# A graph layer and a mixture of experts on one core: an eighth of the edges' table rows fetched by TensorE instead of by GpSimd, with changes in the head, the router, the experts and the last stage

## The chip, the cores and the metric

The kernel runs on one core of a Trainium2 chip. The metric is the device time of one execution in microseconds (us), median of the runs. All data are float32 where nothing else is said.

## The reference, cut to what matters

x has 6250 nodes of 256 features, src and dst are 200,000 edges sorted by dst, edge_attr_2 gives two weights for each edge.

```python
def _L0_gnn_ref(h, adj, direction, W_forward, W_reverse, attn_forward):
    h_fwd = h @ W_forward.T                # 64 columns
    h_rev = h @ W_reverse.T                # 64 columns
    src, dst = (adj[0], adj[1])
    messages = h_fwd[src] * direction[:, 0:1] + h_rev[src] * direction[:, 1:2]
    scores = jnp.einsum('ef,hf->eh', messages, attn_forward[0])      # 4 heads
    scores = jax.nn.leaky_relu(scores, negative_slope=0.2)
    exp_scores = jnp.exp(scores - scores.max(axis=0, keepdims=True))
    sum_exp = jax.ops.segment_sum(exp_scores, dst, num_segments=N)
    norm = exp_scores / (sum_exp[dst] + 1e-10)
    outs = [jax.ops.segment_sum(messages * norm[:, hd:hd + 1], dst, num_segments=N) for hd in range(H)]
    return jnp.stack(outs, axis=1).reshape(N, -1)
...
x = x + _L0_gnn_ref(_layernorm(x), ...)
# 16 experts, the two best per node, hidden size 512, with biases, then a layer norm with gamma and beta
x = x + _L0_ffn_ref(_layernorm(x)[None], ...)[0]
```

## The kernel before

The work goes in five stages. TensorE, VectorE, ScalarE, GpSimd (with its own DMA queue) and SyncE (which issues most other DMAs) each run a hand-written list of instructions, ordered only by semaphores; the order in a list is the order in the code.

**Head** (`stage_edges`, first half, L211 to L622). The nodes are 49 tiles of 128 (NT). x is loaded to token_rows in eight parts, two in flight. For each tile TensorE transposes x (L397), ScalarE copies it (L330), TensorE multiplies it with the weights (L407), and ScalarE (L340) and VectorE (L505) in turn scale the product with 1/deviation to a row of 136 numbers: 64 and 4 (scores of the heads) for the forward matrix, the same for the reverse one. The tiles of a part are stored to the table in HBM, node_table, from two buffers. VectorE takes statistics (L482), converts dst and takes its ranges in each unit of 256 edges (L546 to L550) between the tiles. Behind the table it works out window starts in one partition (L569 to L622); the operation of L622 sets the semaphore `prepared`.

**Edges** (L625 to L851). 196 chunks (NCH) of 1024 edges, 8 columns (K) of 128 edges; four chunks (RING) are in flight. Per chunk: SyncE loads the indices; GpSimd issues eight indirect DMAs, one for each column, each of which gathers 128 rows of 136 numbers from node_table (L203 to L208, waiting at L705 to L707 for indices and for the buffer). ScalarE multiplies the reverse part (L723), VectorE the forward part (L770), both form scores (L773 to L787) and messages (L797), ScalarE the exponential (L728). VectorE forms a one-hot of the destination in a window of 16 nodes (hot, L779) and multiplies it with the exponentials (hot_ex, L801). TensorE sums a chunk's messages into 4 windows by 8 products (L688), which VectorE adds to the sums in SBUF (acc, L763) one chunk later, after it has loaded the windows' positions into registers. The loop body has four chunks.

**Nodes** (`stage_nodes`): seven groups of seven tiles: the sums are divided, x is added, a layer norm is made (xn), xn is transposed and multiplied with the gate weights, VectorE finds the two best experts and a slot for each (slot_i), and GpSimd scatters each row twice (98 indirect DMAs, L1011) to `dispatched` in HBM.

**Experts** (`stage_experts`): 104 tiles of 128 rows of one expert each; SyncE loads the expert's first weights, the rows xs (L1423) and the second bias, broadcast to all partitions (L1425); TensorE transposes (L1501) and makes both layers (L1512, L1522); VectorE adds the bias (L1577) and weighs (L1582); GpSimd scatters the result (L1375) to expert_rows.

**Last stage** (L1595 to L1747): for each group both rows of a node are loaded and added, normalised, scaled with gamma and stored, with two buffers; gamma is loaded behind the first group's rows (L1664).

## Time and profile before

| | |
|---|---|
| median of 3 runs | 2765.64 us (2764.18 to 2768.57) |
| the profiled execution: its own time | 2765.15 us |
| the profiled execution: span, first to last instruction | 2763.0 us |
| instructions | 40,902 |
| GpSimd busy | 1794.8 us |
| VectorE busy | 1178.0 us |
| TensorE busy (matmul) | 943.2 us |
| ScalarE busy | 757.5 us |
| HBM read, written | 222.54 MB, 38.69 MB |

The table by stretch gives busy times of each engine in a piece of the span, the granted clock of TensorE as a share of 2.4 GHz (0.50 is 1.2 GHz) and the mean load of the 16 DMA engines. The groups of instructions give, for one line of the kernel, the busy time and the mean duration of one, and the idle time of the engine just before them with what ended it. "PE" is TensorE, "PEld" its weight loads, "DVE" VectorE, "ACT" ScalarE, "POOL" GpSimd, "SP" SyncE; "issue" is time in which an engine waited for nothing that the profile shows.

### The profile page before, as it was taken

The numbers are of one execution on the slowest core, as the hardware profiler recorded it, in microseconds if no ns is written. First come the engines' busy times: TensorE is split into PE (matmuls) and PEld (weight loads), VectorE is DVE, ScalarE is ACT, GpSimd is POOL, SyncE is SP. The second block draws the span as 40 slices with busy tenths as digits, with TensorE's granted clock in tenths as the row PEclk, the third lists the DMA queues.
The fourth block names the chain that finished last, engine by engine and source line by source line (L and its number), as shares of the span: only waits on it lengthen the run. The fifth ranks groups of instructions, "written<-read, shape, count | busy, mean of one in ns | idle before, by whom it ended". The sixth has DMA issues, their size and how long they took to land.

```text
span 2763.0 us, 40902 instructions
## 1 busy us (share of the span) xinstructions
PE 943.2 (34%) x6693; PEld 862.8 (31%) x6694; DVE 1178.0 (43%) x4381; ACT 757.5 (27%) x2809; POOL 1794.8 (65%) x1923
## 2 busy tenths in 40 slices
PE   6311222222222211122222222211126559899860
PEld 6211111111111111111111111111126458888850
DVE  5533333333333333333333333333347656666646
ACT  3222222222222222222222222222234323333334
POOL 3677777777777777777777777777735643333326
PEclk8555555555555555555555555555555579999985
DMA  5222222222222222222222222222212667676656
GB/s 170 60 57 56 56 57 56 56 57 56 56 57 56 56 57 56 56 56 56 56 57 56 57 56 56 57 56 56 57 28 78 216 204 222 213 220 217 218 183 225
DMA packets 191305, 260.90 MB, mean 94 GB/s; under 512 B 64374, under 2 KB 133047, under 8 KB 191140
## 3 DMA queue, kind: packets, MB, share of 16 engines
q0 software_dynamic: 59872, 135.05, 19.8%
q1 hardware_dynamic: 124980, 122.05, 14.4%
q10 hardware_dynamic: 6416, 3.41, 0.4%
q8 instruction: 11, 0.18, 0.0%
q14 instruction: 26, 0.21, 0.0%
HBM read 222.54 MB, written 38.69 MB: 95 GB/s over the span
## 4 chain that ended last, share of the span: by engine, by line
POOL 53%; issue 21%; PE 8%; DMA 6%; DVE 5%; SPq 4%; ACT 2%; POOLq 1%; DVEq 0%; ACTq 0%
POOL rows L206 52%; DMA xs<-dispatched 4%; SPq L1366 3%; PE p_y L1522 2%; PE p_h L1512 2%; PE p_l L1093 1%; POOL dispatched L1011 1%; ACT xn L1043 1%; PE p_tab L407 1%; DMA shared<-expert_rows 1%; DMA dispatched<-xn,slot_i 1%; ACT staged L1027 1%; PE p_t L1108 1%; PE p_x L1501 0%; SPq L1416 0%
## 5 line engine op out<-in xcount | busy, mean ns | idle before, releaser
L206 POOL DMA_INDIRECT rows<-node_table,index x1568 | 1480.2, 944 | 533.0 <-issue 477.3
L688 PE MATMUL p_win<-hot_ex,msg 128*65 128x64 f32 x3136 | 393.8, 319 | 1559.2 <-DVE hot_ex L801 1170.5
L688 PEld LDWEIGHTS p_win<-hot_ex,msg 128*65 128x65 f32 x3136 | 359.6, 229 | 1593.3 <-issue 1187.6
L723 ACT ACTIVATE p_part<-rows,attr_all 128x64 f32<-128x64 f32 x1568 | 388.4, 299 | 1495.2 <-DMA rows<-node_table,index 1495.2
L770 DVE TENSOR_TENSOR part<-rows,p_attr 128x544 f32<-128x544 f32 x196 | 141.3, 721 | 870.4 <-DMA rows<-node_table,index 868.8
L763 DVE TENSOR_TENSOR shared<-shared,p_win 65x64 f32 x784 | 171.0, 218 | 394.4 <-issue 312.7
L1375 POOL DMA_INDIRECT expert_rows<-ys,back x104 | 102.0, 981 | 308.6 <-DVE ys L1582 240.9
L1512 PEld LDWEIGHTS p_h<-xt,shared 128*128 128x128 f32 x1664 | 203.4, 193 | 5.4
L1512 PE MATMUL p_h<-xt,shared 128*128 128x128 f32 x1664 | 203.9, 276 | 0.0
L1522 PE MATMUL p_y<-shared,hid_t 128*128 x832 | 197.6, 381 | 0.0
L1522 PEld LDWEIGHTS p_y<-shared,hid_t 128*128 128x128 f32 x832 | 149.9, 190 | 16.3
L1011 POOL DMA_INDIRECT dispatched<-xn,slot_i x98 | 99.4, 1014 | 77.2 <-issue 41.5
L797 DVE TENSOR_TENSOR msg<-part,p_part 128x512 f32<-128x512 f32 x196 | 132.6, 677 | 0.0
L801 DVE TENSOR_TENSOR hot_ex<-hot,p_ex 128x512 f32<-128x512 f32 x196 | 132.6, 677 | 0.0
L1467 ACT ACTIVATE hid_t<-p_h,shared 128x128 f32<-128x128 f32 x208 | 64.9, 363 | 174.2 <-PE p_h L1512 174.1
L1548 DVE TENSOR_SCALAR hid_t<-p_h,shared 128x128 f32<-128x128 f32 x208 | 63.4, 346 | 96.4 <-PE p_h L1512 94.6
L1577 DVE TENSOR_TENSOR p_y<-p_y,b_t 128x256 f32<-128x256 f32 x104 | 45.0, 432 | 54.6 <-PE p_y L1522 54.0
L1501 PE MATMUL p_x<-ident,xs 128*128 128x128 f32 x208 | 42.0, 284 | 70.8 <-DMA xs<-dispatched 70.8
L1485 ACT ACTIVATE own<-xs,is_first 128x256 f32<-128x256 f32 x104 | 52.6, 506 | 27.2 <-DVE is_first L1559 25.9
L1582 DVE SCALAR_TENSOR_TENSOR ys<-p_y,weight,own 128x256 f32<-128x256 f32 x104 | 50.3, 484 | 20.8 <-DVE p_y L1577 20.6
L1454 ACT ACTIVATE xt<-p_x 128x256 f32<-128x256 f32 x104 | 39.9, 383 | 62.8 <-PE p_x L1501 62.8
L779 DVE TENSOR_TENSOR hot<-dst_rel,p_dve 128x128 f32<-128x128 f32 x196 | 54.8, 280 | 0.0
(221 smaller groups left out, 1254.0 us busy)
## 6 DMA issues: line engine op xcount, KB each, us to landing
shared<-in_w SPq DMA_DIRECT2D x120, 512.0 KB, 6.3
rows<-node_table,index POOLq DMA_INDIRECT x1568
xs<-dispatched SPq DMA_DIRECT2D x104, 129.5 KB
b_t<-in_b SPq DMA_DIRECT2D x104, 128.0 KB, 4.1
shared<-expert_rows SPq DMA_DIRECT2D x14, 768.0 KB, 6.3
out<-shared SPq DMA_DIRECT2D x6, 896.0 KB, 4.1
token_rows<-in_x SPq DMA_DIRECT2D x5, 896.0 KB, 7.2
index<-in_src SPq DMA_DIRECT2D x196, 4.0 KB, 1.6
```

The costliest lines, as they stand in the source:

```text
L206: pool.indirect_dma_start(out=rows[:, s, k, :], out_offset=None, in_=table, in_offset=bass.IndirectOffsetOnAxis(ap=index[:, s, k:k + 1], a ...
L688: last = pe.matmul(psum[0:MSG, u * HEADS * W:(u + 1) * HEADS * W], msg[:, v, k, :], weighted[:, k, :, :].rearrange("p h w -> p (h w)"), st ...
L723: last = act.activation(p_part[:, v, k, :], rows[:, s, k, COLS:COLS + HD], ACT.Copy, scale=attr_all[:, 1, ds(c * K + k, 1)])
L763: return dve.tensor_tensor(to, to, psum.rearrange("p (h w) -> p h w", h=HEADS), ALU.add)
L770: dve.tensor_tensor(part[:, :, :], rows[:, s, :, 0:COLS], attr_p[:, 0, :].unsqueeze(2).broadcast_to([P, K, COLS]), ALU.mult)\
L797: dve.tensor_tensor(msg[:, v, :, 0:HD], part[:, :, 0:HD], p_part[:, v, :, :], ALU.add)\
L801: dve.tensor_tensor(hot_ex[:, v, :, :, :], hot[:, :, :].unsqueeze(2).broadcast_to([P, K, HEADS, W]), ex_p.unsqueeze(3).broadcast_to([P, K, ...
L1011: pool.indirect_dma_start(out=dispatched, out_offset=bass.IndirectOffsetOnAxis(ap=slot_i[:, v, n:n + 1], axis=0), in_=xn[:, v, n // 2, :], ...
L1366: return nc.values_load_multi_w_load_instructions(of[:, ds(i * R5 + first, n)], engines=[eng.engine], min_val=0, max_val=most)[1]
L1375: pool.indirect_dma_start(out=expert_rows, out_offset=bass.IndirectOffsetOnAxis(ap=back[:, r, :], axis=0), in_=ys[:, r, :], in_offset=None ...
L1512: last = pe.matmul(p_h[:, u, f // 2, (f % 2) * P:(f % 2 + 1) * P], w1_r[:, r % R5, c, f * P:(f + 1) * P], xt[:, u, c, :], start=(c == 0), ...
L1522: last = pe.matmul(p_y[:, u, 0:D], hid_t[:, u, c, :], w2_sb[:, ds(e, 1), c, :] .rearrange("p a d -> p (a d)"), start=(c == 0), stop=(c == ...
```

## The change

In the edge stage the eighth column (k = 7) of each chunk isn't gathered. The table stays in SBUF too (tab, in the memory of token_rows, 51 tiles of 136 numbers for each partition). SyncE writes the eighth column's sources, reduced to a third of the table, as `keys` to HBM once, and loads them for four chunks at a time, broadcast to all partitions. For each chunk VectorE compares the 128 keys with the node numbers of 17 tiles (GP = 17, onehot, 17 blocks of 128 x 128, in two pieces of 9 and 8 blocks). TensorE makes 17 products of a block with 3 x 136 = 408 columns of tab, all added up in one PSUM tile p_hot (`fetch`). The 408 columns are the row's candidates from the three thirds of the table. ScalarE writes the first, times a 0/1 mask, to the rows buffer (`keep_first`), VectorE adds the other two (`keep_others`). The last chunk gathers fewer columns. x is overwritten by this, so it is loaded again behind the last fetch.

Head: all tiles of the table stay in SBUF, x is loaded with four parts in flight, tiles are transposed in pairs and copied out in threes; the ranges of the destinations are made after the table; GpSimd makes keys and masks before it clears acc; 16 transposes of the identity run on TensorE at the start. Router: gate weights are centred, x before the layer norm is transposed and the logits are scaled with 1/deviation afterwards; the loop is unrolled, and the work of a group is spread otherwise. Experts: all second biases lie in SBUF, the 104 broadcasts of b2 go. Last stage: three load buffers, a first group of three tiles, three of seven additions on GpSimd instead of four of seven, other order.

```diff
-PARTS = [0, 2, 5] + [2 + U * m for m in range(1, NG)] + [NT]
+TRIPLE = 3
+PARTS = [0, 3] + list(range(6, NT, 6)) + [NT]
...
+KG = K - 1
+KG_LAST = -(-(EDGES - (NCH - 1) * CHUNK) // P)
+GP = -(-NT // 3)
+LEAD = 2
...
+        over_x = token_rows[:, :, :].rearrange("p t d -> p (t d)")
+        ends = [3 * GP * ROW, 3 * GP * ROW + 2 * GP * P, 3 * GP * ROW + 2 * GP * P + RING * P]
+        tab = over_x[:, 0:ends[0]].rearrange("p (t r) -> p t r", r=ROW)
+        onehot = over_x[:, ends[0]:ends[1]].rearrange("p (v g e) -> p v g e", v=2, g=GP)
+        key = over_x[:, ends[1]:ends[2]].rearrange("p (s e) -> p s e", s=RING)
...
-        def gather(pool, s):
-
-            for k in range(K):
+        def gather(pool, s, count=KG):
+
+            for k in range(count):
                 pool.indirect_dma_start(out=rows[:, s, k, :], out_offset=None, in_=table,
...
             @block.sync
             def _(sp):
                 def step(c, s, it, _):
-                    after(sp, gathered[s], 16 * K * it)
+                    after(sp, gathered[s], 16 * KG * it)
                     sp.dma_start(index[:, s, :], src[c] if isinstance(c, int)
                                  else src[ds(c, 1)].rearrange("a p k -> (a p) k")).then_inc(index_ready[s], 16)
 
-                chunks(sp, lambda it: None, step, RING)
+                def begin(it):
+
+                    if isinstance(it, int) and it == 0:
+                        return
+                    sp.wait_ge(hot_built, 2 * RING * it)
+                    of = keys[it * RING:(it + 1) * RING, :] if isinstance(it, int) else keys[ds(it * RING, RING), :]
+                    sp.dma_start(key[:, :, :], of.partition_broadcast(P)).then_inc(key_ready, 16)
+
+                chunks(sp, begin, step, RING)
...
              @block.scalar
             def _(act):
...
-                    act.wait_ge(gathered[s], 16 * K * (it + 1))
+                    act.wait_ge(gathered[s], arrived(c, s, it))
+                    act.wait_ge(hot_kept, 2 * (c + 1))
...
+                    if follows(c, 1):
+                        keep_first(c + 1, (s + 1) % RING)
+
+                def keep_first(c, s):
+
+                    act.wait_ge(hot_rows, c + 1)
+                    after(act, rows_used, c - RING + 1)
+                    act.activation(rows[:, s, KG, :], p_hot[:, 0:ROW], ACT.Copy, scale=third[:, 0, ds(c, 1)])\
+                       .then_inc(hot_third, 1)
...
              @block.tensor
             def _(pe):
...
+                    if follows(c, LEAD):
+                        fetch(c + LEAD, s % LEAD)
+
+                def fetch(c, v):
+
+                    after(pe, hot_kept, 2 * c)
+                    for gr in range(GP):
+                        if gr % HALF == 0:
+                            pe.wait_ge(hot_built, 2 * c + 1 + gr // HALF)
+                        last = pe.matmul(p_hot[:, 0:3 * ROW], onehot[:, v, gr, :], tab[:, gr:3 * GP:GP, :],
+                                         start=(gr == 0), stop=(gr == GP - 1))
+                    last.then_inc(hot_rows, 1)
...
              @block.vector
             def _(dve):
...
                     extra_windows(c, s, loaded[s])
+                    if follows(c, 1):
+                        keep_others(c + 1, (s + 1) % RING)
+                    if follows(c, LEAD):
+                        build_hot(c + LEAD, (s + LEAD) % RING, it + (s + LEAD) // RING)
+
+                def build_hot(c, s, it):
+
+                    dve.wait_ge(key_ready, 16 * (it + 1))
+                    after(dve, hot_rows, c - 1)
+                    for a, b in ((0, HALF), (HALF, GP)):
+                        dve.tensor_tensor(onehot[:, s % 2, a:b, :],
+                                          key[:, s, :].unsqueeze(1).broadcast_to([P, b - a, P]),
+                                          group_p[:, a:b].unsqueeze(2).broadcast_to([P, b - a, P]), ALU.is_equal)\
+                           .then_inc(hot_built, 1)
+
+                def keep_others(c, s):
+
+                    dve.wait_ge(hot_third, c + 1)
+                    row = rows[:, s, KG, :]
+                    for m in range(1, 3):
+                        after(dve, hot_kept, 2 * c + m - 1)
+                        dve.scalar_tensor_tensor(out=row, in0=p_hot[:, m * ROW:(m + 1) * ROW],
+                                                 scalar=third[:, m, ds(c, 1)], in1=row, op0=ALU.mult, op1=ALU.add)\
+                           .then_inc(hot_kept, 1)
...
 +            sp.wait_ge(g["hot_rows"], NCH)
+            for i in range(NG):
+                v, n = reloaded(i)
+                sp.wait_ge(v, n - 16)
+                if i == NG - 1:
+                    sp.wait_ge(s_hm, 1)
+                sp.dma_start(token_rows[:, i * U:(i + 1) * U, :],
+                             g["x"][i * U * P:(i + 1) * U * P, :].rearrange("(u p) d -> p u d", p=P)).then_inc(v, 16)
...
                     for c in range(KC):
                         last = pe.transpose(p_t[:, u % 2, c * P:(c + 1) * P],
-                                            xn[:, v, u, c * P:(c + 1) * P], ident[:, :])
+                                            tile_row(token_rows, t, c * P, P), ident[:, :])
...
 -                after(sp, s_ys, j - R5 + 1)
-                sp.dma_start(b2_t[:, r, :], g["b2"][ds(e, 1), :].rearrange("a d -> (a d)")
-                             .partition_broadcast(P)).then_inc(s_b2[r], 16)
...
-                dve.tensor_tensor(p_y[:, r % 2, 0:D], p_y[:, r % 2, 0:D], b2_t[:, r, :], ALU.add)\
+                dve.tensor_tensor(p_y[:, r % 2, 0:D], p_y[:, r % 2, 0:D], tile_row(b2_sb, e), ALU.add)\
                    .then_inc(s_biased, 1)
...
 +        LOADED, STORED, KEPT, SUMS = 3, 2, 4, 4
+        spots = [0, 3] + [3 + U * m for m in range(1, NG)] + [NT]
+        on_pool = [len(ts) * 3 // U for ts in tiles]
```

## Rows read from the trace of the kernel before

**Rows 1.** The page: busy times, and TensorE's clock in 40 slices

```profile
PE 943.2 (34%) x6693; PEld 862.8 (31%) x6694; DVE 1178.0 (43%) x4381; ACT 757.5 (27%) x2809; POOL 1794.8 (65%) x1923
...
PEclk8555555555555555555555555555555579999985
```

**Rows 2.** Busy time by stretch: stretch, length, engines, PEclk, DMA share, GB/s

```profile
500.00:1000.00 500.00, 100.44 (x800) 91.74 (x800) 174.54 (x601) 115.57 (x503) 378.10 (x401) 0.50 0.25 56
...
2300.00:2400.00 100.00, 90.72 (x619) 84.12 (x618) 62.96 (x264) 38.58 (x120) 32.54 (x36) 1.00 0.69 217
```

**Rows 3.** Groups by form, 1000 to 1100 us (line, busy, mean ns, idle before)

```profile
L206 POOL DMA_INDIRECT rows<-node_table,index x81 | 76.4, 943 | 24.7 <-issue 24.7
L723 ACT ACTIVATE p_part<-rows,attr_all 128x64 f32<-128x64 f32 x82 | 20.4, 299 | 76.7 <-DMA rows<-node_table,index 76.7
...
L763 DVE TENSOR_TENSOR shared<-shared,p_win 65x64 f32 x40 | 8.7, 218 | 20.1 <-issue 16.1
...
L801 DVE TENSOR_TENSOR hot_ex<-hot,p_ex 128x512 f32<-128x512 f32 x10 | 6.8, 677 | 0.0
L779 DVE TENSOR_TENSOR hot<-dst_rel,p_dve 128x128 f32<-128x128 f32 x11 | 3.1, 279 | 0.0
```

**Rows 4.** The chain that ended last, expert stage (start, us, what)

```profile
2243.10 1.73 PE p_y L1522 x8
2244.83 1.78 PE p_h L1512 x16
```

**Rows 5.** Instructions in order of time, end of the head

```profile
82.40 1.51 PE L440 MATMUL p_b<-lohi,ones 1*128 1x392 f32 x2
...
94.98 0.16 DVE L622 COPY neg_shift<-p_d 128x1 f32<-128x1 f32 x1 [0.67 <-PE p_d L448]
```

**Rows 6.** Groups by form, 0 to 80 us

```profile
L340 ACT ACTIVATE rows<-p_tab,rstd 128x136 f32<-128x136 f32 x25 | 9.3, 373 | 13.6 <-PE p_tab L407 7.6 <-DMA node_table<-rows 5.3
L505 DVE TENSOR_SCALAR rows<-p_tab,rstd 128x136 f32<-128x136 f32 x24 | 8.5, 354 | 21.3 <-DMA node_table<-rows 11.7 <-PE p_tab L407 9.4
```

**Rows 7.** Groups by form, 2260 to 2560 us

```profile
L1582 DVE SCALAR_TENSOR_TENSOR ys<-p_y,weight,own 128x256 f32<-128x256 f32 x72 | 34.8, 484 | 14.9 <-DVE p_y L1577 14.9
```

**Rows 8.** Instructions in order of time, one chunk of the edges

```profile
1004.27 0.68 DVE L801 TENSOR_TENSOR hot_ex<-hot,p_ex 128x512 f32<-128x512 f32 x1
...
1005.19 2.02 PE L688 MATMUL p_win<-hot_ex,msg 128*65 128x64 f32 x16 [8.13 <-DVE hot_ex L801]
```

**Rows 9.** Instructions in order of time, the last chunk

```profile
2040.14 0.72 DVE L770 TENSOR_TENSOR part<-rows,p_attr 128x544 f32<-128x544 f32 x1 [6.81 <-DMA rows<-node_table,index]
...
2048.07 1.27 DVE L763 TENSOR_TENSOR shared<-shared,p_win 65x64 f32 x4 [2.40 <-PE p_win L688]
```

**Rows 10.** GpSimd in order of time, first and last of 98 scatters

```profile
2086.18 1.03 POOL L1011 DMA_INDIRECT dispatched<-xn,slot_i  x1 [35.69 <-DVE slot_i L1189]
...
2226.13 0.97 POOL L1011 DMA_INDIRECT dispatched<-xn,slot_i  x1 [0.31 <-issue]
```

**Rows 11.** Waits from 2240 to 2670 us (total, times, longest)

```profile
PE p_x L1501 <- DMA xs<-dispatched: 37.1, 29, 1.8
```

**Rows 12.** The page: DMA issues (KB each, us to landing)

```profile
b_t<-in_b SPq DMA_DIRECT2D x104, 128.0 KB, 4.1
```

**Rows 13.** VectorE's waits from 2673 to 2763 us

```profile
DVE shared L1721 <- DMA gamma<-in_gamma: 12.5, 1, 12.5
```

**Rows 14.** Busy time by stretches of 5 us, head and expert stage (as rows 2)

```profile
55.00:60.00 5.00, 2.47 (x19) 1.95 (x18) 4.68 (x17) 1.91 (x7) 0.00 (x0) 0.96 0.25 75
60.00:65.00 5.00, 4.88 (x27) 4.64 (x28) 2.28 (x9) 2.52 (x7) 0.00 (x0) 0.69 0.08 25
...
2235.00:2240.00 5.00, 3.42 (x15) 3.02 (x16) 0.00 (x0) 2.03 (x3) 0.00 (x0) 0.50 0.47 128
2240.00:2245.00 5.00, 5.00 (x37) 4.79 (x36) 2.33 (x16) 2.57 (x10) 0.00 (x0) 0.92 0.64 156
...
2275.00:2280.00 5.00, 3.16 (x24) 2.83 (x24) 3.88 (x18) 1.50 (x5) 2.36 (x3) 1.00 0.70 219
```

More of the change, by code:

```diff
@@ L386, in _, with transpose, product @@
                 last.then_inc(s_wp, 1)
+                def transpose(q):
+                    after(pe, s_xtc, q - 2)
+                    for t in pair(q):
+                        pe.wait_ge(s_x[part_of[t] % 4], 16 * (part_of[t] // 4 + 1))
+                        for c in range(KC):
+                            at = (t % 2) * D + c * P
+                            last = pe.transpose(p_xt[:, q % 3, at:at + P], token_rows[:, t, c * P:(c + 1) * P],
+                                                ident[:, :])
+                    last.then_inc(s_xt, 1)
+                def product(t):
+                    q, j, m = t // 2, t // TRIPLE, t % TRIPLE
+                    pe.wait_ge(s_xtc, q + 1)
+                    if t == 0:
+                        pe.wait_ge(s_wd, 2)
+                    if m == 0 and j >= 3:
+                        copies, n = copied(j - 2)[0 if by_act(j) else 1]
+                        pe.wait_ge(copies, n)
+                    for c in range(KC):
+                        last = pe.matmul(p_tab[:, j % 3, m * ROW:(m + 1) * ROW], x_tr[:, q % 3, t % 2, c, :],
+                                         w_all[:, c, :], start=(c == 0), stop=(c == KC - 1))
+                    if t == triple(j)[-1]:
+                        last.then_inc(s_tab, 1)
+                transpose(0)
                 pe.wait_ge(s_ident, 3)
@@ L1057, in deviation @@
                 act.activation(rstd[:, :], mv[:, :, 1], ACT.Sqrt, bias=eps[:, 0:1]).then_inc(s_sd, 1)
-            stage(0)
+            stage(0, 0, U)
+            transposed(0)
+            stage(1, 0, GB)
             deviation(0)
-            alternate(act, step)
-            totals(NG - 1)
+            normalised(0, 0, 0)
+            unrolled(act, step)
         @block.tensor
         def _(pe):
+            pe.wait_ge(s_in, 32)
+            for c in range(KC):
+                last = pe.matmul(p_n[:, 0, 0:E], ones[:, :], gate_w_sb[:, c, :], start=(c == 0), stop=(c == KC - 1))
+            last.then_inc(s_gs, 1)
             pe.wait_ge(s_hm, 1)
@@ new lines, in store @@
+            def store(n):
+                sp.wait_ge(s_f, spots[n + 1])
+                for a, b, real in pieces(n):
+                    sp.dma_start(dram(g["out"], a, b, real),
+                                 out_rows[0:real, n % STORED, a - spots[n]:b - spots[n], :])\
+                      .then_inc(s_out[n % STORED], 16)
+            sp.wait_ge(returned, 1)
+            load(0)
+            sp.dma_start(gamma[:, :], g["gamma"].partition_broadcast(P)).then_inc(s_g, 16)
+            for n in range(1, LOADED):
+                load(n)
@@ L1673, in _ @@
+            for n in range(count):
+                if n + LOADED < count:
+                    load(n + LOADED)
+                store(n)
+            for n in range(count - STORED, count):
+                sp.wait_ge(s_out[n % STORED], stored(n))
         @block.scalar
         def _(act):
[L1675 to L1679 removed]
@@ new lines, in _ @@
+            act.wait_ge(returned, 1)
+            act.activation(table_for[:, :], eps[:, :], ACT.Sqrt)
+            second_rows(0)
+            deviation(0)
+            for n in range(count):
+                if n + 1 < count:
+                    second_rows(n + 1)
+                act.wait_ge(s_rc, 2 * n + 2)
+                for t in tiles[n]:
+                    u = t - spots[n]
+                    after(act, s_gm, t - KEPT + 1)
+                    act.activation(p_norm[:, t % KEPT, 0:D], y0[:, n % LOADED, u, :], ACT.Identity,
+                                   bias=nmr[:, n % 2, u:u + 1], scale=rstd[:, n % 2, u:u + 1]).then_inc(s_nm, 1)
+                if n + 1 < count:
+                    deviation(n + 1)
```

786 lines of the change are left out of this document (436 added, 350 removed).

## The prediction, made before the kernel was run

> **What bounds the kernel now.** First the page's busy shares and its 40 slices [rows 1]: GpSimd is busy 65% of the span, TensorE 34%, and in the long middle TensorE shows 1 to 2 tenths at half clock (1.2 GHz) and GpSimd 7. The table by stretch [rows 2] shows what the stages are made of: the edges run from 95 to 2049 us [rows 5, 9], then nodes, experts and the last stage take 714 us together. In 500 us of edges GpSimd is busy 378 us and TensorE 100; in experts TensorE is busy 91 us of 100 at full clock (2.4 GHz). The groups of the edge stage [rows 3] say why GpSimd's 76% is its limit: 81 gathers in 100 us, 0.943 us each with 0.305 us of issue between them, 1.248 us a gather, 8 gathers or 9.985 us a chunk. The other engines wait for the gathered rows (ScalarE 76.7 us of 100), and TensorE waits for them in turn. 196 chunks of 9.985 us are 1957 us, and the measured stage has 1954 [rows 5, 9]. So the edges cost 71% of the time, and a gather less per chunk is worth something, if nothing slower takes its place.
>
> **The edges after the change.** Removed: one gather of eight per chunk, 1.248 us x 196 = 244 us on the engine that is now the limit. GpSimd would need 8.74 us a chunk.
>
> Added on TensorE, for each chunk: fetch, 17 products (GP) of a 128x128 one-hot block with 408 columns (3 x 136) of the table, all f32. An f32 product leaves two matmul records in this trace: 4 calls of 256 columns are 8 records in 1.73 us and 8 calls of 128 columns 16 records in 1.78 us, both at full clock [rows 4]. That is 0.216 us per record of 256 columns, 0.845 ns a column. The widest f32 products of the trace, 392 columns at half clock, take 0.85 us a record (two in 1.51 us) [rows 5]: 1.65 ns a column from start to start plus 0.2 us until the end, so twice the above at half the clock. A record of 408 columns is then 0.345 us at full clock, a call 0.69, and a fetch 34 x 0.345 + 0.2 = 11.9 us. This alone is more than the whole chunk costs now (9.985 us). 196 x 11.9 = 2332 us against a stage of 1954.
>
> Can it lie beside the other work? PSUM has one p_hot. The chain from one fetch to the next, by the code: the last product ends; ScalarE copies the first third (136 columns with a scale from PSUM, 0.373 us [rows 6]); VectorE adds the other two thirds, two dependent operations of 136 columns (0.484 us is the one of this form with 256 columns; 120 columns fewer at 1.04 ns are 0.36 [rows 7]); then VectorE, in its own order, builds the next one-hot block, first 9 groups, 1152 elements: hot_ex has 512 elements in 0.677 us and hot 128 in 0.279, so 1.04 ns an element, 1.34 us [rows 3]; then TensorE starts, 0.23 us after VectorE's end as in a chunk now [rows 8]. With 0.04 us at each of three hand-overs and 0.08 of overlap between VectorE's operations: 0.04 + 0.37 + 0.04 + 0.36 + 0.04 + 0.36 - 0.08 + 1.34 + 0.23 = 2.7 us. TensorE's window products (2.0 us a chunk at half clock [rows 8], about 1.1 at full) fit in these 2.7 us; the second 8 groups (1.2 us of VectorE) are built during the first 9 products. **Period: 11.9 + 2.7 = 14.6 us.**
>
> What stays hidden, by what: VectorE has 3.5 us of old work a chunk [rows 2] plus 0.7 and 2.6, in all 6.8 of 14.6; its word load and waits (1.6 us before the four windows [rows 3]) fit in the 11.9 us of a fetch. ScalarE's 8 copies (2.4 us) too. SyncE moves the keys once in four chunks, 256 KB after the fourth build, with a fetch of 11.9 us before they are wanted; the 128 KB broadcast of b2 takes 4.1 us [rows 12], so twice that at worst still fits. Behind this wait on SyncE stand the four index loads, and behind them GpSimd; it has 5.8 us to spare in each period. If the cover of 2.7 us is too thin for windows, branch and the word load in every fourth chunk, it costs up to 1 us a chunk; below, a gap of 2.0 us is the least I can make of the three drains and the build. So the period is between 13.9 and 15.6.
>
> Sum of the stage: first build 1.4 and a first fetch that starts at half clock 14.0 (see the clock below), second fetch 13.2, 194 periods 2832, then the last row's thirds 1.2 and a last chunk as now, 9.2 us [rows 9]: 2871 us for 1954. **+917 us** (bounds +780 and +1110).
>
> **The other parts.** Head: VectorE waits 11.7 us for table stores and 9.4 for products [rows 6]; the new head keeps all tiles of the table in SBUF, so the first wait goes, and part of the second by copies of three tiles at once; but the ranges of the destinations, now made between the tiles, move behind the table. -12 (between -25 and +8). Nodes: 98 scatters from 2086.2 to 2227.1, at 0.97 and 0.31 us of issue each 125 of 141 us [rows 10]; the router starting from unnormalised rows can win the rest and a few us of start, while x comes in again behind the last fetch under a tail of 10 us: -15 (-30 to +10). Experts: without the b2 broadcast, 104 transfers of 128 KB fewer; TensorE waits 37.1 us in all for xs [rows 11], of which I take 15 (0 to -37). Last stage: its start waits 12.5 us for gamma behind the first loads [rows 13]; small first group and third buffer: -10 (0 to -20). Together **-52**.
>
> 2763 + 917 - 52 = 3628 us of span. The profiled execution took 2765.15 with a span of 2763.0, half a microsecond from the median of 2765.64, so 2.6 are added: **3630 us**.
>
> **One rule against the trace.** In the expert stage the clock rose after some 4.2 us of busy TensorE (3.42 in one stretch, 0.8 in the next, whose mean is 0.92), and then stayed at full through a stretch of 5 us with 1.84 us idle; in the head, after a stretch with 2.5 us idle in 5, the mean fell to 0.69 [rows 14]. The new gap has 1.6 us without products (2.7 less 1.1) and 13 us of products around it, so I take full clock throughout. The Trainium skill, TensorE: Matmul & The Clock Gate, section on a second HAM failure mode, reports a kernel in which short idles between groups of matmuls, as buffers in PSUM went round, brought the clock down again and again. By that rule each fetch here would begin slow, which is the first rival below.
>
> **The rivals.**
> (1) The clock falls in each gap. Each fetch then has 4.2 us at half clock and loses 2.1 us: 194 x 2.1 = 407, **4040 us**. For it: the fall in the head [rows 14]. Against: the expert stage, whose idles are as long, keeps full clock.
> (2) The clock stays at half in the edges, as it does now [rows 2]. A fetch is 34 x 0.68 + 0.2 = 23.3, the period 26.1, 194 x 11.5 = 2231 more: **5870 us**. Against: TensorE is then busy over 90%, more than in the stretch where it rose.
> (3) The other side: faster. Its place is the fetch on TensorE: if the products with a one-hot block took much less than the two passes of 0.845 ns a column that the rows show, for instance one short pass, and a fetch came under 8.74 - 2.7 = 6.0 us (0.35 us a call), the gathers would bound again: 196 x 8.74 = 1713, -244 - 52, **2470 us**. It breaks even at a period of 10.2 us, a fetch of 7.5 us or 0.44 us a call. Against: 0.69 us a call by two shapes at full clock [rows 4], and the blocks and the table are declared f32.
> That the change doesn't do what it says I give nothing of its own: only the eighth column is fetched in the new way, and the gathers are counted in a loop.
>
> **How the numbers follow.** Forecast 0.83 (own range 3440 to 3850, from the bounds of the stage, less or more the small parts), rival (1) 0.08, (2) 0.05, (3) 0.03, and 0.01 for something that ends within 0.2%, about what a measurement of this kernel can tell from no change. The range 3440 to 4050 takes in rival (1) and leaves out some 0.15. Faster 0.03, same 0.01, slower 0.96.
>
> **What would show it.** GpSimd with 7 gathers a chunk and idle after them, waiting for used rows; TensorE about 87 to 90% busy through the edges at clock 1.0, with 34 records of 408 columns a chunk of some 0.35 to 0.5 us recorded; fetch to fetch 14.6 us, with 2.7 us between, and one-hot builds of 1.34 and 1.2 us; node stage starting near 2950. In the chain, TensorE's fetch line with some 60% of the span instead of GpSimd's gather with 52%. Wrong it would be if the records of 408 columns are spaced under 0.22 us (3), if the clock in the edges is 0.5 (2) or between (1), or if the gap between fetches is over 4 us, which would mean a wait that I haven't seen (keys, or VectorE's old work before the thirds).

## The result and the profile after

The changed kernel takes 3886.56 us (median of 4 runs, 3884.60 to 3886.97) against 2765.66 us: a ratio of 1.4045, interval 1.4023 to 1.4067. The forecast was 3630 us, with a range of 3440 to 4050; the result lies in the range, between the forecast and rival (1), but outside the forecast's own range of 3440 to 3850. The profiled execution has a span of 3882.8 us, 1119.8 more than the kernel before.

Where the time went is read off the boundaries between the stages, in the order of time (start, us, engine, line, operation, and in brackets the idle time before it with what ended it). The end of the head:

```profile
88.12 0.16 DVE L695 COPY neg_shift<-p_tab 128x1 f32<-128x1 f32 x1 [0.67 <-PE p_tab L536]
```

The last addition of a window, which ends the edges:

```profile
3217.30 1.27 DVE L894 TENSOR_TENSOR shared<-shared,p_win 65x64 f32 x4 [2.23 <-PE p_win L781]
```

The first and the last of the 98 scatters of the node stage:

```profile
3247.17 1.04 POOL L1187 DMA_INDIRECT dispatched<-xn,slot_i  x1 [27.45 <-DVE slot_i L1387]
...
3375.26 0.98 POOL L1187 DMA_INDIRECT dispatched<-xn,slot_i  x1 [0.30 <-issue]
```

The first product of the experts, and the last scatter of the experts:

```profile
3392.21 1.11 PE L1699 MATMUL p_x<-ident,xs 128*128 128x128 f32 x4 [48.17 <-DMA xs<-dispatched]
```

```profile
3805.64 0.98 POOL L1576 DMA_INDIRECT expert_rows<-ys,back  x1 [0.94 <-issue]
```

Against the same boundaries of before [rows 5, 9, 10]; its first product of the experts and their last scatter are these:

```profile
2234.92 0.69 PE L1501 MATMUL p_x<-ident,xs 128*128 128x128 f32 x2 [32.10 <-DMA xs<-dispatched]
```

```profile
2673.51 0.97 POOL L1375 DMA_INDIRECT expert_rows<-ys,back  x1 [0.75 <-issue]
```

| stage | before | after | difference | forecast |
|---|---|---|---|---|
| head, to the end of L622 / L695 | 95.1 | 88.3 | -6.9 | -12 |
| edges, to the last window added | 1954.2 | 3130.3 | **+1176** | +917 |
| nodes, to the experts' first product | 185.6 | 173.6 | -12 | -15 |
| experts, to the start of their last scatter | 438.6 | 413.4 | -25 | -15 |
| last stage | 89.5 | 77.2 | -12 | -10 |

So the four small parts give back 56 us, near the 52 forecast, and the whole difference to the forecast lies in the edges. The page of the changed kernel (busy shares, the clock in 40 slices, and the groups that answer to [rows 1, 3]):

```profile
PE 3292.4 (85%) x13377; PEld 2057.2 (53%) x13378; DVE 1756.7 (45%) x5176; ACT 842.2 (22%) x2982; POOL 1608.7 (41%) x1726
...
PEclk8999999999999999999999999999999995599996
...
L873 PE MATMUL p_hot<-token_rows 128*128 128x408 f32 x6664 | 2553.9, 546 | 383.4 <-DVE token_rows L950 382.1
...
L236 POOL DMA_INDIRECT rows<-node_table,index x1368 | 1291.5, 944 | 1839.3 <-DMA index<-in_src 1400.4
L961 DVE SCALAR_TENSOR_TENSOR rows<-p_hot,third,rows 128x136 f32<-128x136 f32 x392 | 140.7, 359 | 1452.8 <-ACT rows L839 1393.0
L839 ACT ACTIVATE rows<-p_hot,third 128x136 f32<-128x136 f32 x196 | 73.2, 373 | 2099.7 <-PE p_hot L873 2099.7
L950 DVE TENSOR_TENSOR token_rows<-token_rows,p_dve 128x1152 f32<-128x1152 f32 (+1 forms) x392 | 485.2, 1280 | 0.0
```

TensorE is busy 85% instead of 34% and its clock is 8 to 9 tenths in the edges, not 5 and not 10. L873 is `fetch`: 196 x 34 = 6664 records, as forecast, but of 546 ns each in the mean; in the second and third experiment below, at full clock throughout, it is 510 and 509. GpSimd (L236) has 1368 gathers instead of 1568 and waits between them, so it bounds nothing now; its waits are put down to the indices, but SyncE issues these behind the keys, which wait for the fourth build, and so go at the pace of the fetches. The idle time before a fetch, 383.4 us, has VectorE's one-hot build (L950) as its releaser, 196 times 2.0 us. The table by stretch, 500 us of the edges (columns as [rows 2]):

```profile
500.00:1000.00 500.00, 439.26 (x1566) 250.23 (x1565) 204.62 (x509) 85.67 (x343) 210.47 (x223) 0.93 0.15 35
```

The clock is 0.93 and TensorE has no product in 61 us of 500. That is neither the forecast (1.00) nor rival (2) (0.50). One chunk of the loop in order of time, from the start of a fetch to the start of the next:

```profile
1503.97 13.60 PE L873 MATMUL p_hot<-token_rows 128*128 128x408 f32 x34 [1.89 <-DVE token_rows L950]
...
1517.41 1.11 PE L781 MATMUL p_win<-hot_ex,msg 128*65 128x64 f32 x16
...
1517.87 0.37 ACT L839 ACTIVATE rows<-p_hot,third 128x136 f32<-128x136 f32 x1 [11.24 <-PE p_hot L873]
...
1518.52 0.36 DVE L961 SCALAR_TENSOR_TENSOR rows<-p_hot,third,rows 128x136 f32<-128x136 f32 x1 [8.02 <-ACT rows L839]
1519.03 0.36 DVE L961 SCALAR_TENSOR_TENSOR rows<-p_hot,third,rows 128x136 f32<-128x136 f32 x1 [0.15 <-DVE rows L961]
1519.31 2.48 DVE L950 TENSOR_TENSOR token_rows<-token_rows,p_dve 128x1152 f32<-128x1152 f32 x2
...
1520.70 1.64 PE L873 MATMUL p_hot<-token_rows 128*128 128x408 f32 x3 [2.18 <-DVE token_rows L950]
```

This fetch takes 13.60 us, the pause without products before it was 1.89 us, the one before the next 2.18 us. From the last product to the third on ScalarE, to VectorE's two thirds, to the build, to TensorE: the chain is the one forecast, in this order. Between the end of ScalarE's copy (1518.24) and VectorE's first third lie 0.28 us, and 0.15 us between the thirds. In time order again, the last four chunks, which aren't in the loop, so that every address is a constant:

```profile
3182.02 11.88 PE L873 MATMUL p_hot<-token_rows 128*128 128x408 f32 x34 [1.66 <-DVE token_rows L950]
...
3193.74 1.11 PE L781 MATMUL p_win<-hot_ex,msg 128*65 128x64 f32 x16
...
3193.95 0.37 ACT L839 ACTIVATE rows<-p_hot,third 128x136 f32<-128x136 f32 x1 [9.35 <-PE p_hot L873]
...
3194.35 0.75 DVE L961 SCALAR_TENSOR_TENSOR rows<-p_hot,third,rows 128x136 f32<-128x136 f32 x2 [6.02 <-ACT rows L839]
3195.02 2.48 DVE L950 TENSOR_TENSOR token_rows<-token_rows,p_dve 128x1152 f32<-128x1152 f32 x2
...
3196.51 3.66 PE L873 MATMUL p_hot<-token_rows 128*128 128x408 f32 x10 [1.66 <-DVE token_rows L950]
```

Here the fetch takes 11.88 us, the two thirds run back to back in 0.75, the pause is 1.66 us and the period from fetch to fetch 14.49: the forecast's 11.9, 1.6 and 14.6. The records say what the other 1.7 us of the loop's fetch are. TensorE in stretches of half a microsecond around the start of that fetch (busy us, clock, DMA share, GB/s):

```profile
1503.50:1504.00 0.50, 0.03 (x1) 1.00 0.63 139
1504.00:1504.50 0.50, 0.50 (x2) 0.96 0.01 0
1504.50:1505.00 0.50, 0.50 (x2) 0.50 0.34 78
...
1507.50:1508.00 0.50, 0.50 (x2) 0.63 0.20 44
1508.00:1508.50 0.50, 0.50 (x2) 1.00 0.00 0
```

Products stop at 1502.08 and start at 1503.97. In the first half microsecond of the fetch the clock is 0.96 in the mean, then 0.50, in the last stretch but one 0.63, then full again: some 3.4 us at 1.2 GHz, which cost 1.7. Over the whole stage, 128 of 194 fetches have such a stretch and take 13.6 us, and 66 take 11.9. In all 128 the clock falls 0.1 to 1.4 us behind the fetch's first product, and not in the pause itself. The mean period is 15.93 us.

### The profile page after: what moved, and what is told of

Read it like the earlier page. It is cut to its first block, busy times and chain, and to the rows that moved or that the text cites. A ratio compares the mean times of both kernels' runs of the same rounds, so it can differ in the third digit from the quotient of the medians.

```text
span 3882.8 us, 56640 instructions
## 1 busy us (share of the span) xinstructions
PE 3292.4 (85%) x13377; PEld 2057.2 (53%) x13378; DVE 1756.7 (45%) x5176; ACT 842.2 (22%) x2982; POOL 1608.7 (41%) x1726
## 4 chain that ended last, share of the span: by engine, by line
PE 68%; DVE 16%; issue 6%; DVEq 4%; ACT 3%; SPq 1%; DMA 1%; ACTq 0%; POOL 0%; POOLq 0%
PE p_hot L873 64%; DVE token_rows L950 7%; DVE rows L961 2%; DVEq L1567 2%; ACT rows L839 2%; DVE p_y L1774 1%; PE p_h L1710 1%; SPq L1142 1%; PE p_y L1720 1%; DVE second L1754 1%; DVEq L961 1%; DVE hid_t L1746 1%; DVE back L1759 1%; PE p_tab L488 0%; DMA out<-shared 0%
## 5 line engine op out<-in xcount | busy, mean ns | idle before, releaser
L873 PE MATMUL p_hot<-token_rows 128*128 128x408 f32 x6664 | 2553.9, 546 | 383.4 <-DVE token_rows L950 382.1
L873 PEld LDWEIGHTS p_hot<-token_rows 128*128 128x128 f32 x6664 | 1345.5, 204 | 1490.8 <-issue 1092.7
L236 POOL DMA_INDIRECT rows<-node_table,index x1368 | 1291.5, 944 | 1839.3 <-DMA index<-in_src 1400.4
L961 DVE SCALAR_TENSOR_TENSOR rows<-p_hot,third,rows 128x136 f32<-128x136 f32 x392 | 140.7, 359 | 1452.8 <-ACT rows L839 1393.0
L839 ACT ACTIVATE rows<-p_hot,third 128x136 f32<-128x136 f32 x196 | 73.2, 373 | 2099.7 <-PE p_hot L873 2099.7
L950 DVE TENSOR_TENSOR token_rows<-token_rows,p_dve 128x1152 f32<-128x1152 f32 (+1 forms) x392 | 485.2, 1280 | 0.0
L781 PEld LDWEIGHTS p_win<-hot_ex,msg 128*65 128x65 f32 x3136 | 217.0, 139 | 75.6 <-issue 69.6
L781 PE MATMUL p_win<-hot_ex,msg 128*65 128x64 f32 x3136 | 217.8, 223 | 5.8 <-DVE msg L930 5.8
L1720 PEld LDWEIGHTS p_y<-shared,hid_t 128*128 128x128 f32 x832 | 150.0, 190 | 16.9 <-issue 0.9
L902 DVE TENSOR_TENSOR token_rows<-rows,p_attr 128x544 f32<-128x544 f32 x196 | 140.3, 716 | 1.7 <-issue 1.6
L930 DVE TENSOR_TENSOR msg<-token_rows,p_part 128x512 f32<-128x512 f32 x196 | 132.7, 677 | 0.0
```

Source lines behind the costliest of these rows:

```text
L236: pool.indirect_dma_start(out=rows[:, s, k, :], out_offset=None, in_=table, in_offset=bass.IndirectOffsetOnAxis(ap=index[:, s, k:k + 1], a ...
L781: last = pe.matmul(psum[0:MSG, u * HEADS * W:(u + 1) * HEADS * W], msg[:, v, k, :], weighted[:, k, :, :].rearrange("p h w -> p (h w)"), st ...
L839: act.activation(rows[:, s, KG, :], p_hot[:, 0:ROW], ACT.Copy, scale=third[:, 0, ds(c, 1)])\
L873: last = pe.matmul(p_hot[:, 0:3 * ROW], onehot[:, v, gr, :], tab[:, gr:3 * GP:GP, :], start=(gr == 0), stop=(gr == GP - 1))
L902: dve.tensor_tensor(part[:, :, :], rows[:, s, :, 0:COLS], attr_p[:, 0, :].unsqueeze(2).broadcast_to([P, K, COLS]), ALU.mult)\
L930: dve.tensor_tensor(msg[:, v, :, 0:HD], part[:, :, 0:HD], p_part[:, v, :, :], ALU.add)\
```

## The experiments

Theory A, of the 259 us that the edges take beyond the forecast: two things lengthen the period, and nothing else. The masks of the thirds are addressed by a register in the loop (`third[:, m, ds(c, 1)]`), which stretches the hand-overs of ScalarE and VectorE and so the pause; and TensorE's clock falls behind most of these pauses. Theory B: something else holds the chain up (keys, VectorE's old work, the build), and the clock only follows it.

**Is it the clock?** Five products that nobody reads, into a free part of the other window tile, behind each chunk's window products:

```diff
+                    for _ in range(5):
+                        pe.matmul(p_win[:, 1 - v, 384:512], ones[:, :], ident[:, :], start=True, stop=True)
                     if follows(c, LEAD):
                         fetch(c + LEAD, s % LEAD)
```

> Edit: after the window sums of each chunk TensorE makes five more f32 products of the ones and the identity (128 columns each, into an unused part of the other p_win bank, read by nobody), so that its pause before the next fetch shrinks from 1.9 us to about 0.9. Theory A: the clock falls in two fetches of three because TensorE pauses 1.9 us and more before each; with shorter pauses every fetch takes 11.9 us instead of 13.6 in 128 of 194, the period is 14.8 us and the time 3887 - 218 = 3670 us. Theory B: the clock falls for another reason (the long load itself, the gathers beside it); then two thirds of the fetches still take 13.6 us and the time stays at 3887, or above it if the products delay the fetch.

Measured: 3671.47 us (3670.93 to 3671.95), ratio 1.3268 [1.3248, 1.3289]. In order of time:

```profile
1509.11 1.11 PE L781 MATMUL p_win<-hot_ex,msg 128*65 128x64 f32 x16
...
1510.05 1.33 PE L865 MATMUL p_win<-ident,ones 128*128 128x128 f32 x10
...
1512.11 11.91 PE L875 MATMUL p_hot<-token_rows 128*128 128x408 f32 x34 [0.72 <-DVE token_rows L952]
```

The ten records of L865 add 1.33 us of work on TensorE, leave a pause of 0.72 us, and the kernel is 215 us faster. All 194 fetches take 11.9 us, and the mean period is 14.82. The period fell by 1.11 us, and 1.11 x 194 = 215 us: the cost of the clock alone, measured. The chain between fetches is untouched (0.52 us from ScalarE's start to VectorE's first third, as without the products).

**Is it the register address?** The same masks with a constant column. Most chunks then take the mask of another chunk, so the eighth column's rows are not the table's; the operations and their sizes are the same.

```diff
-                                   scale=third[:, 0, ds(c, 1)])
+                                   scale=third[:, 0, s:s + 1])
...
-                                                 scalar=third[:, m, ds(c, 1)], in1=row, ...)
+                                                 scalar=third[:, m, s:s + 1], in1=row, ...)
```

> Edit: the masks of keep_first and keep_others are read at a fixed column of third instead of one computed from the chunk's number, so the loop computes no address between the end of a fetch and the next build; the masks are then those of four chunks, so the eighth column's rows are taken from the wrong third (this part of the computation is changed). Theory A (register work stretches the hand-overs, the pause grows from 1.66 to 1.9 and 2.2 us, and only the longer pause lets the clock fall): pause 1.66 us as in the unrolled first and last chunks, all fetches 11.9 us, period 14.5, time 3887 - 194 x 1.43 = 3610 us. Theory B (the clock falls for another reason): period shorter by 0.3 us only, two thirds of the fetches 13.6 us, time about 3830 us.

Measured: 3599.24 us (3597.97 to 3602.31), ratio 1.3005 [1.2985, 1.3025]. In order of time:

```profile
1520.89 0.37 ACT L839 ACTIVATE rows<-p_hot,third 128x136 f32<-128x136 f32 x1 [9.30 <-PE p_hot L873]
...
1521.30 0.75 DVE L961 SCALAR_TENSOR_TENSOR rows<-p_hot,third,rows 128x136 f32<-128x136 f32 x2 [5.88 <-ACT rows L839]
1521.97 2.47 DVE L950 TENSOR_TENSOR token_rows<-token_rows,p_dve 128x1152 f32<-128x1152 f32 x2
...
1523.36 7.80 PE L873 MATMUL p_hot<-token_rows 128*128 128x408 f32 x22 [1.57 <-DVE token_rows L950]
```

In the loop the hand-overs are now as in the chunks outside it: VectorE's thirds start 0.41 us behind ScalarE's start (0.65 in the chunk of the changed kernel that is shown, 0.52 in most), both take 0.75 us in one piece instead of 0.87, and the pause is 1.57 to 1.66 us. The mean period is 14.45 us, and the clock never falls: 194 of 194 fetches take 11.91. Against the kernel with the added products this is 0.37 us a period less, 72 us in all: the price of the register addresses by themselves. Their second price is the clock, since with them the pause is 1.9 us, without them 1.6. It is the pause and not the address that matters to the clock: the kernel with the added products has the register addresses and a short pause, and its clock doesn't fall either.

**What does the build in the chain cost?** VectorE builds the block of two chunks ahead before it takes the thirds, not behind them:

```diff
-                    if follows(c, 1):
-                        keep_others(c + 1, (s + 1) % RING)
                     if follows(c, LEAD):
                         build_hot(c + LEAD, (s + LEAD) % RING, it + (s + LEAD) // RING)
+                    if follows(c, 1):
+                        keep_others(c + 1, (s + 1) % RING)
```

> Edit: at the end of a chunk's step VectorE builds the one-hot block of chunk c+2 before it adds the thirds of chunk c+1, not after. The build then lies beside the fetch of c+1. Theory A (the chain from fetch to fetch holds 1.34 us of build, and pauses under some 1.7 us keep the clock): period 14.8 - 1.34 = 13.5 us, all fetches 11.9 us, time 3887 - 194 x 2.43 = 3415 us. Theory B (the clock falls also so): period 14.6, time 3630 us. Theory C (the build isn't in the chain): no change, 3887 us.

Measured: 3433.73 us (3433.35 to 3438.49), ratio 1.2408 [1.2389, 1.2427]. In order of time:

```profile
1506.51 0.36 DVE L961 SCALAR_TENSOR_TENSOR rows<-p_hot,third,rows 128x136 f32<-128x136 f32 x1 [4.75 <-ACT rows L839]
1507.02 0.36 DVE L961 SCALAR_TENSOR_TENSOR rows<-p_hot,third,rows 128x136 f32<-128x136 f32 x1 [0.15 <-DVE rows L961]
...
1507.52 11.91 PE L873 MATMUL p_hot<-token_rows 128*128 128x408 f32 x34 [0.71 <-DVE rows L961]
...
1512.87 2.47 DVE L950 TENSOR_TENSOR token_rows<-token_rows,p_dve 128x1152 f32<-128x1152 f32 x2
```

The build (L950 at 1512.87) now lies beside the fetch, the thirds are the last link, the pause is 0.71 us and the clock stays at 1.00. The mean period is 13.59 us. Against the kernel with the added products that is 1.22 us less, 238 us in all, for the 1.34 us that theory A expected. But 11.9 us of products alone are still more than the 9.985 us of eight gathers.

**What are the other parts worth?** The fetch is undone: GpSimd gathers all eight columns (three in the last chunk, which has no more edges), there are no keys, builds or thirds; all else is as in the changed kernel.

> Edit: the changed kernel with the eighth column gathered by GpSimd again, and without keys, builds, fetches and thirds; head, second load of x, router, experts and last stage stay as changed. If the fetch alone made the kernel slower: edges back at 1954 us, the other stages -56 us by the two traces (head -7, nodes -12, experts -25, last -12), time 2710 us. If a part of these 56 us hangs on the changed edges (a load of x that is hidden only behind the last fetches, the clock with which TensorE enters the nodes), the time is nearer to 2766.

Measured: 2694.95 us (2694.62 to 2696.99), ratio 0.9741 [0.9728, 0.9754]. 500 us of the edges (columns as [rows 2]):

```profile
500.00:1000.00 500.00, 100.48 (x800) 91.72 (x800) 174.64 (x603) 114.94 (x500) 377.81 (x402) 0.50 0.26 56
```

These are the numbers of the kernel before [rows 2]: GpSimd 377.81 us of 500, TensorE 100 at half clock. The head, router, experts and last stage of the change are worth 2.6% when the fetch is left out. It is 72 us faster than the kernel before on the same chip (2767.37). In its own trace the small parts give 55 and the edges the other 16 (1938.6 for 1954.2). Of these 16, 5 gathers less in the last chunk are 5 x 1.25 = 6. Most of the rest belongs to the new head: the first gather starts at 64.4 us instead of 78.2, which is 24.6 us ahead of the end of the head (as the table above draws it) instead of 16.9.

**Was rival (3) priced rightly?** The fetch makes 3 of its 17 products, so that most rows of the eighth column are missing; builds, thirds and waits are all there.

```diff
                     for gr in range(GP):
                         if gr % HALF == 0:
                             pe.wait_ge(hot_built, 2 * c + 1 + gr // HALF)
+                        if 1 < gr < GP - 1:
+                            continue
```

> Edit: a fetch makes 3 of its 17 products (the eighth column's rows come out wrong for most nodes: 14 of 17 blocks are left out), all else as in the changed kernel: keys, builds, thirds, seven gathers. It asks what lies under the fetch. Theory A: under 6 us of fetch the gathers bound again, 7 x 1.248 = 8.74 us a chunk; edges 1713 us, time about 2695 - 225 = 2470 us. Theory B: VectorE's own list bounds (6.5 us busy a chunk, 1.6 us for loading words, and the waits for ScalarE and TensorE in keep_others); then the period is 9.3 us or more and the time 2580 or more, near or above the kernel with eight gathers (2695) if it comes to 10 us. A rest of the clock's fall can't matter to A: three products at half clock take 4.2 us.

Measured: 2485.47 us (2483.20 to 2486.07), ratio 0.8977 [0.8962, 0.8992]. 500 us of the edges, and GpSimd's gathers from 1000 to 1500 us:

```profile
500.00:1000.00 500.00, 313.03 (x1260) 186.50 (x1259) 371.77 (x914) 151.64 (x627) 377.78 (x402) 0.70 0.28 64
```

```profile
L236 POOL DMA_INDIRECT rows<-node_table,index x401 | 378.3, 943 | 122.2 <-issue 114.0 <-DVE p_dve L907 4.9 <-ACT p_part L825 3.4
```

401 gathers in 500 us are 57.3 chunks of 8.73 us, with little but issue between them (114.0 of 122.2 us): the gathers bind at seven a chunk, as rival (3) said (8.74, 2470 us). So the idea has room, and what it lacks is a cheap fetch. VectorE, now at 372 us of 500, is not far from binding too.

**A fetch that is cheap.** The blocks are 0 and 1, which bf16 holds exactly. The table is kept as two bf16 words, the upper half of each f32 and the rest, split in place by one subtraction on VectorE in the head. The 17 f32 products become 34 in bf16 (the order of the build is as in the third experiment). The row that is fetched has then some 16 bits of the table's 24.

```diff
+        tab_b = over_x[:, 0:ends[0]].bitcast(BF16).rearrange("p (t r b) -> p t r b", r=ROW, b=2)
...
+                dve.tensor_tensor(tab_b[:, :, :, 0], tab[:, :, :], tab_b[:, :, :, 1], ALU.subtract)
...
-                        last = pe.matmul(p_hot[:, 0:3 * ROW], onehot[:, v, gr, :], tab[:, gr:3 * GP:GP, :],
-                                         start=(gr == 0), stop=(gr == GP - 1))
+                        for b in range(2):
+                            last = pe.matmul(p_hot[:, 0:3 * ROW], onehot[:, v, gr, :], tab_b[:, gr:3 * GP:GP, :, b],
+                                             start=(gr == 0 and b == 0), stop=(gr == GP - 1 and b == 1))
```

> Edit, with the build before the thirds as in the run with that name: the one-hot blocks are bf16, and each f32 word of the table in SBUF is split in place into its upper half and the bf16 of the rest (one VectorE operation of 6936 elements, about 7.3 us, behind the stores of the table), so that a fetch is 17 x 2 bf16 products of 408 columns, one record each. Theory A: a bf16 record takes half of an f32 one, 0.17 us at full clock, a fetch 5.9 us (7.7 with the clock's fall), and the period comes to the gathers' 8.74 us or VectorE's list, 8.8 to 9.4: time 2465 to 2590 us. Theory B: TensorE now pauses so long in each period that the clock stays at half; a fetch takes 11.8 us, the period is 13.4 and the time about 3370 us. Theory C: the stride of two in the table's columns makes a record as long as an f32 one; fetch 11.9, time about 3430 us.

Measured: 2615.43 us (2610.93 to 2620.22), ratio 0.9444 [0.9428, 0.9459]: faster than the kernel before, and 25 us above the upper end of theory A, whose mechanism the trace bears out. In order of time:

```profile
1003.86 0.36 DVE L967 SCALAR_TENSOR_TENSOR rows<-p_hot,third,rows 128x136 f32<-128x136 f32 x1 [0.15 <-DVE rows L967]
1004.25 0.72 DVE L908 TENSOR_TENSOR token_rows<-rows,p_attr 128x544 f32<-128x544 f32 x1
...
1004.35 6.29 PE L879 MATMUL p_hot<-token_rows 128*128 128x408 bf16 x34 [1.50 <-DVE rows L967]
...
1012.59 0.36 DVE L967 SCALAR_TENSOR_TENSOR rows<-p_hot,third,rows 128x136 f32<-128x136 f32 x1 [0.15 <-DVE rows L967]
...
1014.87 0.72 DVE L908 TENSOR_TENSOR token_rows<-rows,p_attr 128x544 f32<-128x544 f32 x1 [1.93 <-issue]
```

34 records take 6.29 us (5.9 expected) where the f32 fetch has 34 in 11.9. The thirds end at 1004.22 and VectorE goes on with the next chunk at once (L908): its own list is the bound now, 8.73 us from L967 to L967. But once in four chunks it stands still for 1.93 us, as before 1014.87: there the loop's body begins, and by the code VectorE loads the words of the next four chunks into registers. It is the load and not the jump of the loop: ahead of chunk 192, the first of the four that stand behind the loop, VectorE stands still for 1.88 us as well. The thirds just before it are short and wait for a semaphore, so nothing covers the load; the next experiment tries this reason. That stall is 0.5 us of the mean period of 9.4. The other 0.2 is the clock: the run shows it falling again, 146 of the 194 fetches have a pause of 1.7 us or less and all take 6.3 us, and of the 48 with a pause of 1.9 us, 46 take 7.8 or more. These 46 are the ones behind the stall, and there VectorE has to wait for the fetch:

```profile
1023.72 7.80 PE L879 MATMUL p_hot<-token_rows 128*128 128x408 bf16 x34 [1.91 <-DVE rows L967]
...
1032.17 0.36 DVE L967 SCALAR_TENSOR_TENSOR rows<-p_hot,third,rows 128x136 f32<-128x136 f32 x1 [0.65 <-ACT rows L844]
```

The period that begins with such a fetch takes 9.53 us in the mean, not 8.73.

**The stall covered.** The second half of the build goes behind the thirds (the last argument names the half that is built):

```diff
                     if follows(c, LEAD):
-                        build_hot(c + LEAD, (s + LEAD) % RING, it + (s + LEAD) // RING)
+                        build_hot(c + LEAD, (s + LEAD) % RING, it + (s + LEAD) // RING, (0,))
                     if follows(c, 1):
                         keep_others(c + 1, (s + 1) % RING)
+                    if follows(c, LEAD):
+                        build_hot(c + LEAD, (s + LEAD) % RING, it + (s + LEAD) // RING, (1,))
```

> As the kernel with the bf16 fetch, with VectorE's list of a chunk as: first half of the one-hot build (9 groups), the two thirds, second half (8 groups). Theory A: in that kernel the period was 8.73 us, VectorE's list without a gap, and every fourth chunk lost 1.9 us, because the word load of the next four chunks came right behind the two short thirds, which wait for a semaphore, so nothing covered it. With 1.2 us of building behind the thirds it is covered: the stall falls from 1.9 us to about 0.7 or less, 49 x 1.2 = 59 us less than 2615, and perhaps the other part too: 2490 to 2560. The bound is then VectorE's list (8.7 us) and the seven gathers (8.74 us) together. Theory B: the load waits for whatever VectorE still has in its queue, and the stall stays: 2615 again. Theory C: the products start sooner than their rows are taken, the hand-over is longer, as the second half now stands behind the thirds in the way of the next products: TensorE waits for VectorE 1.2 us more a chunk, which it can afford (fetch 6.3 and windows 1.1 of 8.7), so this changes nothing until it exceeds 1.3 us.

Measured: 2531.45 us (2530.44 to 2535.47), ratio 0.9150 [0.9137, 0.9162]. VectorE at the start of the loop's body:

```profile
1221.17 0.35 DVE L970 SCALAR_TENSOR_TENSOR rows<-p_hot,third,rows 128x136 f32<-128x136 f32 x1
...
1221.94 1.21 DVE L959 TENSOR_TENSOR token_rows<-token_rows,p_dve 128x1024 bf16<-128x1024 f32 x1
1224.05 0.72 DVE L908 TENSOR_TENSOR token_rows<-rows,p_attr 128x544 f32<-128x544 f32 x1 [0.90 <-issue]
```

The stall is 0.90 us instead of 1.93, and the mean of 56 chunks in 500 us (392 gathers by 7) is 8.93 us, for 9.4. This saved 84 us, more than the 49 x 1.03 = 50 of the shorter stall alone. The clock in the edges, 0.98 for 0.95, goes with it: the fetch behind the stall now follows a pause of 0.8 us and is slow 18 times instead of 46, and the period that begins with it takes 8.91 us in the mean instead of 9.51, so 49 x 0.6 = 29 us more. This version is 235 us faster than the kernel before on the same chip, and within 46 us of the run with 3 products, which the seven gathers bound.

## Why the prediction was right, and where it was off

**The bound and the direction** were right: the gather saved per chunk is worth nothing, since a fetch of 11.9 us replaces 9.985 as the bound. Undoing the fetch alone brings 3887 us down to 2695.

**The fetch**, 34 x 0.345 + 0.2 = 11.9 us, priced from records of 128, 256 and 392 columns: it takes 11.88 to 11.91 us at full clock.

**The gap** of 2.7 us, term by term: ScalarE 0.37 (0.37), VectorE's thirds 0.36 each (0.36), the first part of the build 1.34 (1.34; both take 2.48), the period where addresses are constant 14.49 (14.6). Window products 1.11 (1.1), the pause there 1.66 (1.6).

**The step that failed** is "The new gap has 1.6 us without products (2.7 less 1.1) and 13 us of products around it, so I take full clock throughout." It failed in two links. First, 1.6 us holds only with constant addresses; in the loop the thirds' masks are addressed by a register, and the pause is 1.9 us, in every fourth chunk 2.2. I had costed the operations by their durations and each hand-over by 0.04 us; the register's part stood in no term. Second, at 1.9 us and more the clock is not safe: 188 of the 194 fetches have such a pause, and it fell in 128. With 1.66 us or less it fell never (194 of 194 in the second experiment). The witness for full clock was the expert stage's 1.84 us [rows 14], which is one pause, the longest of that stage:

```profile
2279.69 0.44 PE L1501 MATMUL p_x<-ident,xs 128*128 128x128 f32 x2 [1.84 <-DMA xs<-dispatched]
```

The clock did stay at 1.00 there. But one pause that keeps the clock is a weak witness: in the changed kernel 60 of the 188 kept it as well.

The range held with some luck. The edges took 1176 us more, above the bound of 1110, since the period of 15.93 us lies above its bound of 15.6; the result is 37 us over the own range that carried 0.83, and inside 4050 only because the stated range took in rival (1), at 0.08. Two sums are a little off: the own range's upper end is 2763 + 1110 + 8 + 10 + 3 = 3894 by the terms given (edges, head, nodes, and what lies outside the span), not 3850, and rival (2) comes to 3630 + 2231 = 5861, not 5870. Neither changes the reading.

The sum closes: 194 x (15.93 - 14.82) = 215 us for the clock, 194 x (14.82 - 14.45) = 72 us for the addresses, less 194 x (14.6 - 14.45) = 29 us for a gap forecast a little too long, is +258 us; the edges came out 259 above the forecast.

**Rival (1)** had the right mechanism at 0.08, too low. It was priced at 2.1 us a fetch in all 194; it is 1.70 us, and in two of three. The Trainium skill, TensorE: Matmul & The Clock Gate, section on a second HAM failure mode, which I weighed and set aside, tells of short idles between groups of matmuls that bring the clock down again and again. The trace agrees, 128 times of 194, and it shows where it stops agreeing: with the same groups and pauses of 1.66 us, none.

**Rival (2)**, half clock throughout, is wrong (0.93 in the edges). **Rival (3)** was wrong for f32 and its price was right: with 3 products the kernel takes 2485 us for 2470, and with bf16 products 2531.

**The small parts.** Head -6.9 for -12. Nodes -12 for -15: the scatters take 129.1 us for 140.9 and begin 8 us sooner after the edges, but the first rows of the experts come 16.0 us after the last scatter, not 7.8, which gives 8 back. Experts -25 for -15: behind its first product TensorE doesn't wait for the rows any more (it was 37.1 us [rows 11]), and the transfers of the bias are gone; which of the two gave it I didn't try. Last stage -12 for -10.

## What to carry to other kernels

Before work is moved from a saturated engine to an idle one, price the whole period of the new engine, its work plus the hand-overs until it can start again, against the one that it replaces: here 14.5 us against 9.985. Of the f32 versions tried the best still has 13.59, and its products alone take 11.9. Then look at what the moved work needs: a 0/1 matrix doesn't need f32. With the build out of the chain the f32 fetch loses 24%, and its bf16 form gains 5.6%, or 8.5% with the stall covered; 2.6% of that gain is what the other parts of the change give without any fetch. And keep pauses of TensorE in a loop short, by taking builds, address registers and word loads out of the chain between its bursts: the address registers cost 72 us by themselves here and 215 more by the clock.

## What the runs showed of the hardware that I had not expected

- A pause of 1.9 us between bursts of 13 us can cost TensorE 3.4 us at 1.2 GHz near the start of the next, 1.70 us net, and it does so in two of three; pauses of 1.57 to 1.66 us did not do it once in 194. In the last kernel 18 of 194 fetches were slow too (7.67 to 7.90 us), behind a pause of 0.8 us; all 18 are at the same place of the loop's body, the first fetch to start behind the word load's stall. Before the one at 1016.90 us TensorE had also stood 1.38 us ahead of its window products, but so it had before the one at 1053.20, which took 6.29. So the pause just before isn't the whole rule, and I leave the rule open.
- Five needless products a chunk, 1.33 us of work, make a kernel 215 us faster.
- A column addressed by a register costs 0.15 us between two dependent operations of VectorE that else run back to back, and some 0.37 us over the three operations of this chain.
- A product in f32 leaves two records, 0.345 us each for 408 columns; a bf16 record of as many columns takes (6.29 - 0.2) / 34 = 0.18. So an f32 product costs nearly as much as four in bf16 (0.69 us for 0.18), and the split into two bf16 parts half of f32.
